# A one-row clear on GpSimd ahead of each indirect DMA of the expert stages

## The reference

```python
x = x + attn_a(layernorm(x))     # linear attention, running sums over time
x = x + ffn(layernorm(x))        # experts
x = x + attn_b(layernorm(x))     # mix with a decayed running sum, gate, project
x = x + ffn(layernorm(x))        # experts again, with the same weights

def ffn(x):                      # 8 experts, 128 -> 512 -> 128
    logits = x @ router_W + router_b
    probs = softmax(logits)
    top1 = argmax(probs)
    h = relu(x @ W1[e] + b1[e])
    y = h @ W2[e] + b2[e]
    out = probs[top1] * y[top1]  # only the chosen expert's result counts
```

## Time and profile before

| | us |
|---|---|
| median of 3 runs | 346.27 |
| lowest and highest run | 344.20 and 346.51 |
| the profiled execution, whole | 345.94 |
| its span, first to last instruction | 344.1 |

### The profile page before, as it was taken

How to read it: one execution, slowest core, us unless ns; L and a number is a source line. 1 busy time by engine, 2 the same in 40 slices (tenths; PEclk the granted TensorE clock), 3 DMA queues, 4 the chain that set the end, 5 groups by cost and what they waited for, 6 DMA issues and landing times.

```text
span 344.1 us, 7662 instructions
## 1 busy us (share of the span) xinstructions
PE 295.8 (86%) x2177; PEld 257.4 (75%) x2177; DVE 243.3 (71%) x1012; ACT 182.8 (53%) x545; POOL 210.9 (61%) x244
## 2 busy tenths in 40 slices
PE   7999999899976599999998997888885599999970
PEld 7566666675866599999964885766875599999970
DVE  4878998878761577777726998889573368777750
ACT  3765555321854376667613752634663376676730
POOL 4954487886485455655545857788575536565560
PEclk9999999989996899999999998999996889999995
DMA  7999211002323443221108001112313344221000
GB/s 195 257 332 144 34 40 33 31 32 58 73 63 88 94 92 91 65 57 32 32 11 236 1 1 33 40 39 71 81 41 86 93 89 104 73 55 41 31 8 1
DMA packets 32521, 25.64 MB, mean 75 GB/s; under 512 B 6000, under 2 KB 28785, under 8 KB 32480
## 3 DMA queue, kind: packets, MB, share of 16 engines
q1 hardware_dynamic: 27328, 16.51, 21.0%
q0 software_dynamic: 4576, 8.54, 7.5%
q10 hardware_dynamic: 576, 0.10, 0.2%
HBM read 14.57 MB, written 11.53 MB: 76 GB/s over the span
## 4 chain that ended last, share of the span: by engine, by line
PE 54%; POOL 10%; DVE 10%; issue 8%; ACT 6%; another core or an unknown queue 6%; DMA 1%; POOLq 0%; ACTq 0%; SPq 0%; DVEq 0%
PE pair L1498 18%; PE pair L1484 13%; POOL sorted L490 6%; PE bank L1484 6%; PE bank L1474 3%; DVE stats L797 2%; POOL rows L464 2%; PE pair L1358 2%; PE pair L1311 2%; ACT hT L741 2%; PE pair L1322 2%; PE pair L1277 1%; PE pair L1350 1%; PE pair L1333 1%
## 5 line engine op out<-in xcount | busy, mean ns | idle before, releaser
L1498 PE MATMUL pair<-w2s,hT 128*128 x624 | 87.0, 285 | 1.4 <-issue 1.1
L490 POOL DMA_INDIRECT sorted<-rows,place x64 | 67.5, 1055 | 28.2 <-issue 20.1
L1498 PEld LDWEIGHTS pair<-w2s,hT 128*128 128x128 f32 x624 | 79.6, 200 | 1.9 <-issue 1.6
L1146 DVE SCALAR_TENSOR_TENSOR ys<-pair,xs 128x128 f32<-128x128 f32 x78 | 27.3, 350 | 53.2 <-PE pair L1498 29.5
L1484 PE MATMUL pair<-xsT,w1s 128*128 128x128 f32 x432 | 61.3, 280 | 1.3 <-ACT xsT L736 1.3
L503 POOL DMA_INDIRECT x_mid<-ys,xs x39 | 41.2, 1056 | 33.2 <-DVE ys L1146 31.1
L503 POOL DMA_INDIRECT out<-ys,xs x39 | 41.1, 1055 | 33.2 <-DVE ys L1146 30.4
L1484 PEld LDWEIGHTS pair<-xsT,w1s 128*128 128x128 f32 x432 | 55.4, 196 | 2.1 <-issue 0.9
L736 ACT COPY xsT<-bank 128x128 f32<-128x128 f32 x78 | 20.8, 267 | 64.0 <-issue 34.1
L660 ACT COPY w1s<-w1all 128x516 f32 x78 | 49.5, 635 | 3.0 <-DVE etab L1074 1.9
L1484 PE MATMUL bank<-xsT,w1s 128*128 128x128 f32 x192 | 30.6, 294 | 12.9 <-ACT xsT L736 12.5
(11 more groups left out here) (164 smaller groups left out, 495.0 us busy)
## 6 DMA issues: line engine op xcount, KB each, us to landing
xs<-sorted SPq DMA_DIRECT2D x78, 66.0 KB
w1all<-in_L_ffn_W_b SPq DMA_DIRECT2D x8, 258.0 KB
rows<-in_L_attn_a_x SPq DMA_DIRECT2D x8, 256.0 KB, 4.1
w2s<-in_L_ffn_W SPq DMA_DIRECT2D x8, 256.0 KB, 6.5
rows<-x_mid SPq DMA_DIRECT2D x8, 256.0 KB, 4.3
sorted<-pad SPq DMA_DIRECT2D x30, 66.0 KB, 3.5
sorted<-rows,place POOLq DMA_INDIRECT x64
x_mid<-ys,xs POOLq DMA_INDIRECT x39
```

Source lines behind the costliest of these rows:

```text
L490: pool.indirect_dma_start(sorted_rows[l], bass.IndirectOffsetOnAxis(ap=place[:, t:t + 1], axis=0), rows[:, t, :], None).then_inc(s_sent[l] ...
L1146: nc.vector.scalar_tensor_tensor(out=ys[b][:], in0=bank[6 + i % 2][:, 0:P], scalar=xs[b][:, GATE:GATE + 1], in1=xs[b][:, 0:D], op0=ALU.mul ...
L1498: mm = nc.tensor.matmul(bank[6 + i % 2][:, 0:P], hT[i % NB][:, c], w2s[:, bass.ds(e, 1), c, :].rearrange("p o d -> p (o d)"), start=(c == ...
```

## The change

A row of 320 numbers in one partition, `idle_row`, is allocated; nothing reads it. POOL clears it before each of the 39 scatters of a layer and before each of the four sends of group 7. Each clear waits for the semaphore count of the clear before it. The four sends are written out (`rows_ready`, then `send_tile` for each tile) where before `send` did the same. The sends of groups 0 to 6 are as before. Nothing else is changed.

```diff
+PAUSE = 320
...
+        idle_row = sb("idle_row", [1, PAUSE])
...
+        s_pause = sem("s_pause")
...
+            def pause(n):
+
+                after(pool, s_pause, n)
+                nc.gpsimd.memset(idle_row[:], 0.0).then_inc(s_pause, 1)
+
             def experts(l):
+                pauses = itertools.count(l * (ST + GT))
                 for i in range(ST):
+                    pause(next(pauses))
                     scatter(l, i)
                     if i == PLACE_AT:
-                        for g in ROUTE_BATCHES[LASTB]:
-                            send(l, (AS, BS)[l], g)
+                        rows_ready(l, (AS, BS)[l], LASTG)
+                        for t in range(LASTG * GT, NT):
+                            pause(next(pauses))
+                            send_tile(l, t)
```

More of the change, by code:

```diff
@@ L1 @@
+import itertools
 from contextlib import ExitStack
```

## The result

| | before | after |
|---|---|---|
| median, us (20 runs of each, on the same chip) | 345.82 | 343.64 |
| lowest and highest, us | 343.93 and 347.95 | 340.32 and 346.28 |
| the profiled execution, whole, us | 345.94 | 341.82 |
| its span, us | 344.1 | 340.1 |

The ratio of the times is 0.9921, with a 95% interval of 0.9895 to 0.9946. The change makes the kernel faster by 0.8%, that is 2 to 3 us, where 15 had been forecast.

The account below looks back on a forecast made before the run. PE bounds the kernel from slot 10 on; in each layer's first slots a freeze during POOL's DMA strings does. 345.94 - 19.6 + 0.7 + 1.0 + 2.1 = 330.1, or 330.5 us against the median; range 324 to 350.

Parts of the forecast that it names:

- nothing: POOL's strings: the clear runs beside the next DMA's preparation, gap stays near 0.30 us; 347 us, chance 0.13.
- half of it: First slots: the stops break up into shorter ones and the 19.6 us gain becomes about 9; 339 us, chance 0.22.
- The cause: First slots of each layer: engines sharing no data stand still during POOL's close-set DMAs; seven slots take 26.64 and 26.46 us.
- 15.5 by slots, router and table: Slots 3 to 10 without stops: 13.2 us for seven slots, 1.0 for router steps, 1.3 for slot table operations.
- the border: Gap between POOL's DMAs during SP's loads: 0.30 us freezes the engines, 0.59 or more does not.
- the whole 19.6 us: First slots of both layers: 22.1 us gained if the freeze goes, less 2.5 left in place.
- the first stop: Behind group 6's sends, which get no clear: DVE's waits for `ys` of slot 4, 2.5 of 3.7 us left in place.
- (c): What is left of the freeze at a 0.58 us gap: 0.19 us on half of 22 spaced steps, 2.1 us.
- The gap: Between POOL's DMAs in a string: 0.02 + 0.36 + 0.20 = 0.58 us instead of 0.30, step 1.62 instead of 1.28.
- (a): End of each layer: the last two scatters are a string on the ending chain; 0.34 us more each, 0.7 in all.
- (b): POOL falls 10 us behind in the first slots, regains 8.6 over 32 slots; 0.5 us a layer counted, 1.0 in all.
- The freeze stays and the clears prolong it: First slots: a 0.58 us gap acts like 0.30, 22 clears add 7.5 us, layer ends 0.7; 354.5 us, chance 0.21.

Follow-up runs that it names:

- a step of 2.30 us: Changed kernel with clears of 1280 numbers, only before the scatters of slots 0 to 8 and the four sends: 351.32 us, ratio 1.0223 to the kernel before.
- the late lot: Kernel before, without clears; SP starts the loads of slots 9 to 20 only when `ys` of slot 5 is done: 341.48 us, ratio 0.9925.
- the string after 156 us: Changed kernel with clears of 560 numbers and none before the scatters of slots 31 to 38, where a string at 1.28 us returns: 329.85 us, ratio 0.9529.

## Why the prediction was wrong

**The kind was right, the size was not.** The time is 343.64 us where 330.5 was forecast: inside the range, on the faster side by 0.8%. Of the cases, "nothing" (347) is the nearest by the number and "half of it" (339) by the kind, and even that gave too much.

**The cause: right.** Engines that share no data stand still while POOL issues indirect DMAs one right behind the other; how it comes about is open. With a step of 2.30 us the first slots need 16.20 us in both layers, where the prediction had worked out 15.5 by slots, router and table; and 20.7 us went in the two layers, where 19.6 were counted. The Trainium skill, "DMA: Bandwidth & Descriptors", section "Issuing engines are not separate DMA queues", would have a space between the DMAs free nothing, since it charges issuing with no more than a sequencer's own time. The runs go against its use here: at 480 numbers the same DMAs from the same engines take 14.3 us less in the first slots.

**The step that failed: the border.** The prediction said "loads with gaps of 0.30 freeze, loads with 0.59 or more don't", put the change at 0.58, and booked the whole 19.6 us. Of the 20.7 us that a step of 2.30 takes away, 4.3 at most went. The other 16.4 stayed, where the sum had 2.5 for the first stop and 2.1 for its term (c). Two things were wrong in it.
- The gap. It took a computation's lead (0.20) behind the clear and 0.02 ahead of it: 0.58. Measured are 0.35 + 0.17 = 0.52, a step of 1.49 instead of 1.62. The clear itself was right (0.355 for 0.36).
- The border. It was read off a single gap of 0.59 in the earlier trace rows, behind a wait for `ys`. One wide gap doesn't free a string: with 0.74 and 0.30 in turn, the first slots take what they take in after. One wide gap in a stretch at 1.89 a slot said nothing on a string.

What each is worth can be told. With a gap of 0.57 (320 numbers in all partitions) the kernel takes 338.81 us, 4.6 less than before, so a gap of 0.58 is not beyond the border (whether the other partitions have a share in the 4.6 is not shown). With the step that had been forecast, 1.63 in the run with 480 numbers, it takes 331.31, within 1 us of the 330.5, though 3 to 10 give 14.3 us there and not 19.6 less 2.1. The forecast had 1.04 us for a DMA, and in a string it takes 0.97 (its own 1.28 less 0.30 gave 0.98); this and the 0.06 of the gap are the 0.13 us between 1.62 and 1.49, and nearly the whole error. The slope there is some 12 us of time for 0.14 us of step.

**What was to come with it.** (a) The two last scatters: 0.34 us a layer forecast, 0.21 measured, since the step is shorter. (b) POOL 10 us behind: it isn't in after, since the stops that remained gave it time. Where they do go, the lateness is there, and it was undervalued: 1.0 us was counted, 0.7 came at 1.63, but 5.9 at 1.69, with (a) in both. (c) What is left of the freeze: 2.1 us were counted from SP's issues, and it is the 16.4 us above. SP's issues did get quicker: 12 loads take 10.40 us in after, 16.05 in the earlier trace rows. The prediction held that the stops come while SP issues loads; the late lot and the string after 156 us with no load at all show that they come without.

**The rivals.** "The freeze stays and the clears prolong it", 354.5: it was right that 0.58 might lie near the border, wrong that the clears would add their own time: the string gets longer and the stops don't (4.30 and 5.10 us against 2.33, 2.90 and 2.06 in layer 0; 2.94 and 5.08 against 2.97 and 3.71 in layer 1). A kernel slower than before does come from a larger clear, by another way: POOL as the bound. "Half of it", 339: the nearest in kind, stops that remain and are in part shorter. "Doesn't do what it says", 347: its mechanism is not there. The gap grew by 0.22 us, and with all 128 partitions cleared the next DMA starts 0.17 us after the clear all the same.

## What to carry over

When engines that share no data stop together, look for the engine that issues indirect DMAs back to back, and read the step over its whole string, not one gap; here strings of up to 1.5 us a DMA stopped PE's partners, and at 1.63 most of it was gone. The cure has a ceiling of its own: the spaced engine must still get through its list in the time that the others need, so the best spacing is the smallest that ends the stops, and where it is late at the end, the last DMAs of a stage do better without (0.9529 against 0.9652 with 560 numbers). A border that only one row supports is a term with two ends, and a forecast on a steep slope wants a price for both.

## What the runs showed of the hardware

- Indirect DMAs of POOL with a mean step of 1.28 us stop ACT and DVE behind PE's finished matmuls, for up to 5 us in before and, in a longer string, for 10.8 us (the run with 1280 numbers). In before, PE's turn of slot 7 is done at 99.56, and ACT gets it at 105.95. The steps at which the stops go fit an estimate of about 1.6 to 1.75 us of something for each such DMA. A plain backlog, worked off in order, doesn't fit: at 132.95 in that run the string at 1.28 us had six DMAs, so that by the estimate 2 to 3 us were piled up, and the signal came 10.5 us later, 1.8 us after the end of the string's last DMA. What holds the signals back, and where, was not found. Shown is that stops come without SP's loads and without the register loads of PE, ACT and DVE, and that no DMA starts beside a one-partition clear.
- A clear on POOL takes 0.355, 0.491, 0.563, 0.625, 0.758 and 1.157 us for 320, 480, 560, 640, 800 and 1280 numbers in one partition, and 0.396 for 320 in all 128. An indirect DMA starts 0.17 us after it.
- SP's 12 loads of layer 0's second lot take 16.05 us in before, 10.40 in after, and 9.4 to 11.6 in all kernels with a larger step. So its issues are already quick at a step at which ACT's stops remain; whether both have one cause is not shown.
